# Normalising the two heads of a biased attention row on GpSimd and ScalarE at once, in a newly found order of steps

## The chip, the core and the metric

The kernel runs on one core of a Trainium2 chip. A core has TensorE (PE in the profile), VectorE (DVE), ScalarE (ACT), GpSimd (POOL) and SyncE (SP), which here only issues DMAs. The engines run side by side; each takes its own instructions strictly in the order in which they were written, and semaphores hold them back where one needs another's result. The metric is the device time of one launch in microseconds (us). Before the change it is 2065.31 us, the median of 3 runs (2063.07 to 2065.85).

## The reference

Four layers are applied to 8 items of 512 tokens by 256 features, in float32, each to the layer-normalised input and added to it: a causal attention with rotary embedding (16 heads of 16), a gated layer, a biased attention, and the gated layer again.

```python
x = L0_attn_a_x
x = x + _L0_attn_a_ref(_layernorm(x, axis=-1), ...)   # layer 0, causal
x = x + _L0_ffn_ref(_layernorm(x, axis=-1), ...)      # layer 1, gated
x = x + _L0_attn_b_ref(_layernorm(x, axis=-1), ...)   # layer 2, biased
x = x + _L0_ffn_ref(_layernorm(x, axis=-1), ...)      # layer 3, gated
```

The gated layer takes the half of the tokens with the highest gate value, runs an attention over them alone, and writes gate times result back to their places. The change is in the biased attention, 16 heads of 64:

```python
scores = jnp.einsum('bhid,bhjd->bhij', q, k) * scale
rel = jnp.arange(t)[None, :] - jnp.arange(t)[:, None] + (t - 1)
bias = rel_bias[rel]
scores = scores + bias.transpose(2, 0, 1)[None]
attn = jax.nn.softmax(scores, axis=-1)
out = jnp.einsum('bhij,bhjd->bhid', attn, v)
```

## The kernel before

The work is cut into steps, named by kind, item s, layer l and two numbers n and q. Kinds that begin with c_ belong to the causal layer, f_ to the two gated ones, b_ to the biased one. Items overlap: while the biased layer of item s runs, the last gated layer of item s-1 and the causal and first gated layer of item s+1 run between its steps. Only the first two items' first layers and the last item's last layer have little or nothing beside them.

In the biased layer n is one of 8 pairs of heads (128 features). b_q, b_k and b_v project the pair. A row is one of the four tiles of 128 queries (q) against all 512 keys, for both heads of the pair, so there are 4 x 8 x 8 = 256 rows. For each row:

- b_row: PE makes the scores of the two heads (L1669, two matmuls, recorded as four), DVE adds the band of biases and takes the maximum (L1394), negates it (L1399), and ACT takes the exponential in place and its sum (L1203), the two heads one after the other;
- b_nrm: DVE takes the reciprocal of the two sums (L1403); POOL multiplies the row of each head by it, in place, the first head and then the second (L1114), and raises norm_done after the second;
- b_tr: PE waits for norm_done, transposes the row (L1677, four transposes for each head, into two PSUM banks), and ACT copies each bank to PT (L1212).

After four rows b_val multiplies by the values (L1687) and b_y projects the output (L1448). Six rows are held in SBUF in probs; their exponentials, their normalised values and what PE transposes are all the same memory.

In the other layers, DVE takes maxima from PSUM (L1303 causal, L1377 gated), ACT takes exponentials from PSUM (L1176 into PTc, L1183 into PTf), PE makes scores from tiles of 32 rows (L1507, L1531, L1602, L1624), and L955 is a helper that records the matmuls of many steps.

Which step comes next is decided once, when the program is built, by a planner (in_order, L578). WORK gives for each kind of step what it costs on which engine; PLACE gives each step a due time, with a row of numbers for each kind in each stage of the run ("first", "cycle", "last" and so on); of the steps whose inputs are done, the one with the lowest due time is next. All engines, and SP's queue of loads for band and wb, follow this one list, each leaving out the steps in which it has no part. The planner also assigns the 8 PSUM banks, which PE takes back when ACT or DVE has read them. Where it reckons that PE will stand idle for long, the kernel writes filler transposes of an identity (L1464 to L1468); there are 636 of them.

PE works with tiles of several shapes: b_row uses two tiles of 64 rows, b_val two of 64 columns, the causal and gated attention steps tiles of 32, the rest the full array. TILES tells the planner which. Its order of before has 1760 steps with work on PE, in which the shape changes 737 times from one step to the next.

Of the kernel before, what the change touches and what calls it, by code (L numbers as in the profile page):

```python
# [9 lines left out]
ALU = mybir.AluOpType  # L10
# [11 lines left out]
PAIRS = H // 2  # L22
# [68 lines left out]
    "norm": {"b_nrm": 1},  # L91
}


def raised(sem, step):
# [42 lines left out]
    "b_nrm": [("dve", 0.065), ("pool", 0.667), ("pool", 0.667)],  # L138
# [46 lines left out]
def wait_for(x, y):  # L185
# [5 lines left out]
    if x.kind == "f_spread" and y.kind == "f_rank":  # L191
# [7 lines left out]
    ("cycle", "b_k"): [3550, -20290, 1306, 4062, 4436, 4140, 4696, 5305],  # L199
    ("cycle", "b_ln"): [1262],  # L200
    ("cycle", "b_nrm"): [2638, 3695, 3640, 3225, -20356, 4054, 2981, 2909, 4109, 4148, 4021, 2935, 4375, 3948, -23318,
        -23114, 4742, 3629, 5013, -4314, -23816, -10443, -23404, 5301, -23338, 5234, 5291, 5573, 4071, -23111, 5627,
        5525],
    ("cycle", "b_q"): [3196, -17363, 2209, 4150, -23317, -23105, -23313, 3727],
    ("cycle", "b_row"): [3568, 2483, 3386, 3576, -17334, 3747, 2880, 3676, 3538, 4356, 3997, 3970, 4036, -22757, 3966,
        -23319, 4525, 3836, -25665, -22838, -23399, 5250, -23127, -23029, 4951, 3629, 4299, 5506, 5521, -4078, 5564,
        5149],
    ("cycle", "b_tr"): [3737, 3899, 1936, 4069, 3053, 4259, 4296, 4109, 3959, -22860, 4110, -22481, -22974, 3923, 4021,
        4492, 5069, 5153, -22477, -21082, -22759, 5270, -6484, 5410, -4078, 5475, 5685, 5028, -18270, 5713, 5715,
        5508],  # L210
    ("cycle", "b_v"): [2826, 3562, 4101, 4300, -23336, 4743, -22759, 3751],
    ("cycle", "b_val"): [4383, 3998, -25042, 4071, 4069, 4022, 3918, 3906, 4617, 4618, -23312, -22775, 3980, 4682,
        -22433, 3910, 5411, -465, -18750, 1128, 5520, -15222, 2450, 5594, 5767, -18026, 5803, 5964, 6117, -23816, 6150,
        4297],
    ("cycle", "b_xt"): [3453],
    ("cycle", "b_y"): [6185, 6257, 5046, 6298],
    ("cycle", "c_dk"): [751, 1735],
    ("cycle", "c_dq"): [-9876, 1178],
    ("cycle", "c_hk"): [-25692, -26122],
    ("cycle", "c_hm"): [1900, 2381],  # L220
    ("cycle", "c_k"): [-25283, 1133],
    ("cycle", "c_ln"): [1596],
    ("cycle", "c_m"): [1231, 2224],
    ("cycle", "c_p1"): [1685, 1880, 825, 1812, 1814, 1835, -26435, 1988, 2283, -25667, 2225, 2342],
    ("cycle", "c_p2"): [-25857, -26620, 2189, -25905, 824, 2403, -31973, -25731, -31999, -31998, 824, -21029],
    ("cycle", "c_q"): [-25895, -1117],
    ("cycle", "c_rq"): [-25876, -25667],
    ("cycle", "c_v"): [1822, 1723],
    ("cycle", "c_va"): [2315, -21553, -26065, -25931, -26140, 2122],
    ("cycle", "c_vb"): [2425, 2341, -21554, 2451, 1708, -27849],  # L230
    ("cycle", "c_xq"): [1304, 1931],
    ("cycle", "c_xt"): [-26366],
    ("cycle", "c_y"): [2558, -27782],
    ("cycle", "f_gate"): [-4118],
    ("cycle", "f_gather"): [2758],
    ("cycle", "f_hk"): [-32246],
    ("cycle", "f_hm"): [-26272, 1112],
    ("cycle", "f_k"): [2803],
    ("cycle", "f_ln"): [-26583],
    ("cycle", "f_m"): [2974, 3174],  # L240
    ("cycle", "f_o"): [3364],
    ("cycle", "f_p1"): [2909, 2146, 2968, 2936],
    ("cycle", "f_p2"): [3157, 3207, 2714, 2145],
    ("cycle", "f_part"): [2341],
    ("cycle", "f_q"): [2876],
    ("cycle", "f_rank"): [2715],
    ("cycle", "f_row"): [2637],
    ("cycle", "f_rq"): [2714],
    ("cycle", "f_spread"): [3210],
    ("cycle", "f_v"): [2878],  # L250
    ("cycle", "f_va"): [3304, 3314],
    ("cycle", "f_vb"): [2818, 1878],
    ("cycle", "f_xq"): [2888],
    ("cycle", "f_y"): [3420, -26301],
    ("cycle3", "f_gate"): [6360],
    ("cycle3", "f_gather"): [6449],
    ("cycle3", "f_hk"): [5867],
    ("cycle3", "f_hm"): [6300, 6916],
    ("cycle3", "f_k"): [6624],
    ("cycle3", "f_ln"): [5519],  # L260
    ("cycle3", "f_m"): [6911, 6955],
    ("cycle3", "f_o"): [7115],
    ("cycle3", "f_p1"): [6841, 6842, 6893, 6912],
    ("cycle3", "f_p2"): [6915, 7004, 6752, 6788],
    ("cycle3", "f_part"): [3988],
    ("cycle3", "f_q"): [6615],
    ("cycle3", "f_rank"): [6377],
    ("cycle3", "f_row"): [5019],
    ("cycle3", "f_rq"): [5082],
    ("cycle3", "f_spread"): [6920],  # L270
    ("cycle3", "f_v"): [6818],
    ("cycle3", "f_va"): [7050, 7068],
    ("cycle3", "f_vb"): [6789, 6751],
    ("cycle3", "f_xq"): [6691],
    ("cycle3", "f_y"): [7172, 6817],
    ("first", "b_k"): [-3531, -5724, -3283, 2755, 15934, 11053, 13316, 7847],
    ("first", "b_ln"): [19106],
    ("first", "b_nrm"): [4611, 2091, 1400, 2970, 3511, 5654, 3829, 1690, 13396, 12728, 14614, 13159, 13289, 2911,
        13060, 13182, 10760, 8545, 8998, 14183, 19693, 11177, 12395, 10720, 3549, 18717, 9584, 18285, 13795, 15430,
        1912, -2429],  # L280
    ("first", "b_q"): [-3868, 2912, 9237, 10023, 11107, 15038, 11335, 16171],
    ("first", "b_row"): [2066, -8171, -4615, -4092, 4637, 2120, 11108, -3532, 2394, 11989, 452, 14111, -11398, 2393,
        8880, 2483, 22791, 8981, 8681, 17105, 3780, 2091, 18708, 6192, 7207, 14652, 6343, 20826, -20208, 4895, 2428,
        526],
    ("first", "b_tr"): [9594, 8800, 4897, 6030, 11633, 4802, 11088, 8568, 13585, 11130, 17050, 10988, 11759, 12828,
        2458, 4136, 14548, 8343, 15354, 19160, 9814, 5419, 9782, 13226, -11880, -1040, -13485, 1333, 4379, 2513, 500,
        5883],
    ("first", "b_v"): [1892, 1604, 11176, 13174, 11234, 11205, 9730, -2031],
    ("first", "b_val"): [10070, 10259, 1988, -7921, 12048, 3827, 4102, 10300, 23781, 5884, 9581, 13207, 10682, 9717,
        8728, 8281, 20971, 11416, 19627, 1555, -20843, 3036, 5244, 3443, -2922, 5941, 5044, 3662, 3462, -9064, 1504,  # L290
        2778],
    ("first", "b_xt"): [22969],
    ("first", "b_y"): [6325, -11860, 5440, 710],
    ("first0", "c_dk"): [282, 2428],
    ("first0", "c_dq"): [-456, -545],
    ("first0", "c_hk"): [-25531, 3679],
    ("first0", "c_hm"): [4148, 2481],
    ("first0", "c_k"): [-7624, -69],
    ("first0", "c_ln"): [-171702],
    ("first0", "c_m"): [4163, 5008],  # L300
    ("first0", "c_p1"): [3589, 3764, 3598, 3598, 3583, 3597, 4158, 4157, -161523, 4003, 4374, 4002],
    ("first0", "c_p2"): [3779, 3930, 1994, 4059, 3953, 3597, 3925, 5275, 4394, 2837, 5214, 3732],
    ("first0", "c_q"): [-8701, -161419],
    ("first0", "c_rq"): [-13080, -11293],
    ("first0", "c_v"): [1491, 3301],
    ("first0", "c_va"): [4609, 3463, 4766, 6280, 3950, 5711],
    ("first0", "c_vb"): [5046, 3489, 2415, 6523, 2581, 4747],
    ("first0", "c_xq"): [1538, 3952],
    ("first0", "c_xt"): [3964],
    ("first0", "c_y"): [6944, 3550],  # L310
    ("first0", "f_gate"): [3590],
    ("first0", "f_gather"): [5264],
    ("first0", "f_hk"): [1650],
    ("first0", "f_hm"): [3715, 6506],
    ("first0", "f_k"): [3478],
    ("first0", "f_ln"): [7065],
    ("first0", "f_m"): [6900, 10182],
    ("first0", "f_o"): [13088],
    ("first0", "f_p1"): [4295, 3631, 7445, 4795],
    ("first0", "f_p2"): [1941, 9074, 10136, 9959],  # L320
    ("first0", "f_part"): [8357],
    ("first0", "f_q"): [5263],
    ("first0", "f_rank"): [7410],
# [12 lines left out]
    ("first1", "c_k"): [3874, 2319],
    ("first1", "c_ln"): [-161544],
# [389 lines left out]
def hybrid_kernel(nc, x_in, wqk_a, wv_a, wo_a, w_b, wo_b, band_in, wg_f, wq_f, wk_f, wv_f, wo_f,  # L727
                  cos_in, sin_in, sides_in, out):
    with ExitStack() as ctx:
# [14 lines left out]
        def sem(name):  # L744
            return ctx.enter_context(nc.semaphore(name))
# [1012 lines left out]
```

## Time and profile before

| | |
|---|---|
| median of 3 runs | 2065.31 us (2063.07 to 2065.85) |
| the profiled execution | 2064.3 us, of which 2062.3 us are the span of the profile |
| PE, weight loads of PE | 1996.6 us (97%), 1282.7 us (62%) |
| DVE, ACT, POOL | 1514.8 us (73%), 1155.7 us (56%), 693.0 us (34%) |
| TensorE clock granted | 0.997 of full speed |

Busy times are shares of the span. PE counts as busy while a matmul is under way by the profile's model of its end, and PEld, the loading of the next weights, overlaps it. The engines' shares don't add up to one another, since they run at the same time.

### The profile page before, as it was taken

What the parts mean: (1) busy time and instruction counts of PE and PEld (TensorE: products, weight loads), DVE (VectorE), ACT (ScalarE), POOL (GpSimd) and SP (SyncE); (2) the same over time, 40 slices, a digit from 0 to 9 for tenths busy, and PEclk for the clock granted to TensorE, in tenths of its full rate; (3) what the DMA queues carried; (4) which work ended last, traced back from release to release, by engine and by line L of the source; (5) the groups of instructions that cost most, each with busy time, mean ns of one, the idle gap of its engine ahead of it and who ended that gap; (6) DMA issues with size and microseconds to landing.
All of it is one profiled execution on the core that took longest, in us unless ns stands there. A gap on an engine that the chain in (4) does not pass through costs nothing.

```text
span 2062.3 us, 42104 instructions
## 1 busy us (share of the span) xinstructions
PE 1996.6 (97%) x16080; PEld 1282.7 (62%) x16080; DVE 1514.8 (73%) x4803; ACT 1155.7 (56%) x2578; POOL 693.0 (34%) x879
## 2 busy tenths in 40 slices
PE   8999999999999999999999999999999999999998
PEld 6676666655666555765566555765566655675567
DVE  8977654877868877778778697686876877857446
ACT  2545763766637475474745657465663766627742
POOL 6323242253313342233523333234341243414220
PEclk9999999999999999999999999999999999999999
DMA  3001211120111111121011211012110120102200
GB/s 146 2 1 35 70 60 59 45 90 19 60 31 63 57 35 44 35 84 43 31 37 52 72 42 45 19 60 72 34 62 10 52 90 17 62 16 70 69 1 21
DMA packets 29062, 98.77 MB, mean 48 GB/s; under 512 B 2880, under 2 KB 11200, under 8 KB 28736
## 3 DMA queue, kind: packets, MB, share of 16 engines
q1 hardware_dynamic: 28864, 96.09, 14.0%
q8 instruction: 129, 2.11, 0.4%
q14 instruction: 69, 0.57, 0.1%
HBM read 91.89 MB, written 4.19 MB: 47 GB/s over the span
## 4 chain that ended last, share of the span: by engine, by line
PE 73%; DVE 17%; ACT 6%; issue 2%; POOL 1%; DVEq 0%
PE ps L955 21%; PE ps L1687 10%; PE ps L1448 10%; PE ps L1677 9%; PE ps L1669 8%; DVE ps L1303 5%; DVE probs L1394 5%; PE ps L1531 3%; ACT PTc L1176 3%; PE ps L1636 2%; DVE peaks L1377 2%; PE ps L1624 2%; PE ps L1545 2%; PE ps L1602 2%; PE ps L1507 2%
## 5 line engine op out<-in xcount | busy, mean ns | idle before, releaser
L1114 POOL TENSOR_SCALAR probs<-probs,rtotal 128x512 f32<-128x512 f32 x512 | 345.5, 695 | 556.5 <-DVE rtotal L1403 555.9
L1203 ACT ACTIVATE probs<-probs,peak 128x512 f32<-128x512 f32 x512 | 365.0, 714 | 156.3 <-DVE peak L1399 155.6
L1394 DVE CUSTOM_DVE_ANT_0 probs<-ps,band 128x512 f32<-128x512 f32 x512 | 332.5, 687 | 61.1 <-PE ps L1669 61.1
L1212 ACT ACTIVATE PT<-ps 128x512 f32<-128x512 f32 x512 | 262.4, 618 | 45.7 <-PE ps L1677 45.7
L1677 PE MATMUL ps<-ident,probs 128*128 128x128 f32 x2048 | 249.5, 275 | 1.6 <-POOL probs L1114 1.2
L1677 PEld LDWEIGHTS ps<-ident,probs 128*128 128x128 f32 x2048 | 225.2, 141 | 39.3 <-issue 28.3
L1303 DVE CUSTOM_DVE_ANT_0 ps<-ps,later 128x512 f32<-128x512 f32 (+3 forms) x512 | 232.7, 526 | 16.5 <-PE ps L1507 16.3
L1669 PE MATMUL ps<-KT,QT 64*128 64x512 f32 x1024 | 242.9, 606 | 0.0
L1687 PE MATMUL ps<-PT,Vb 128*64 128x512 f32 x1024 | 239.6, 601 | 0.0
L955 PE MATMUL ps<-xnT,wb 128*128 128x512 f32 x512 | 233.5, 598 | 0.6 <-ACT xnT L1139 0.6
L1176 ACT ACTIVATE PTc<-ps 128x384 f32<-128x384 f32 (+1 forms) x384 | 167.7, 550 | 40.6 <-PE ps L1531 39.8
L1377 DVE TENSOR_REDUCE peaks<-ps 128x2 f32<-128x512 f32 x256 | 156.7, 681 | 21.2 <-PE ps L1602 21.2
L955 PEld LDWEIGHTS ps<-xnT,wb 128*128 128x128 f32 x512 | 93.1, 190 | 108.5 <-issue 100.7
L1106 POOL TENSOR_SCALAR_AFFINE_SELECT PTc<-PTc 128x512 f32<-128x512 f32 x128 | 81.4, 648 | 234.0 <-ACT PTc L1176 233.7
L1669 PEld LDWEIGHTS ps<-KT,QT 64*128 64x128 f32 x1024 | 94.1, 186 | 92.1 <-issue 72.0
L1077 POOL TENSOR_TENSOR rstd<-veps,pow_half 128x2 f32<-128x2 f32 x64 | 46.8, 734 | 308.8 <-DVE veps L1234 308.7
L1183 ACT ACTIVATE PTf<-ps 128x512 f32<-128x512 f32 x256 | 130.4, 616 | 29.4 <-PE ps L1624 28.8
L1687 PEld LDWEIGHTS ps<-PT,Vb 128*64 128x64 f32 x1024 | 65.5, 136 | 126.8 <-issue 113.3
L955 PEld LDWEIGHTS ps<-wb,xnT 128*128 128x128 f32 x1024 | 121.3, 192 | 16.6 <-issue 12.7
L955 PE MATMUL ps<-wb,xnT 128*128 128x128 f32 x1024 | 126.2, 277 | 0.0
L1448 PE MATMUL ps<-wob,OTb 128*128 128x256 f32 x512 | 113.7, 379 | 0.0
L1448 PEld LDWEIGHTS ps<-wob,OTb 128*128 128x128 f32 x512 | 96.4, 190 | 12.6
(156 smaller groups left out, 3348.9 us busy)
## 6 DMA issues: line engine op xcount, KB each, us to landing
band<-in_band SPq DMA_DIRECT2D x64, 896.0 KB, 4.5
wb<-in_w_b SPq DMA_DIRECT2D x64, 384.0 KB, 3.1
x<-in_x SPq DMA_DIRECT2D x16, 256.0 KB, 3.0
out<-x SPq DMA_DIRECT2D x16, 256.0 KB, 2.2
wob<-in_wo_b SPq DMA_DIRECT2D x1, 1024.0 KB, 8.5
wqk<-in_wqk_a SPq DMA_DIRECT2D x1, 512.0 KB, 5.7
cos_t<-in_cos SPq DMA_DIRECT2D x1, 256.0 KB, 5.2
sin_t<-in_sin SPq DMA_DIRECT2D x1, 256.0 KB, 6.1
```

Of the source, the lines that this page charges most:

```text
L955: last = nc.tensor.matmul(o, w, r, start=(i == 0), stop=(i == len(pairs) - 1))
L1114: last = g.tensor_scalar(unit, unit, rtotal[:, r % 8, e:e + 1], 1.0, ALU.mult, ALU.mult)
L1176: a.activation(pt_c(m, q)[:, h], bank(now, name)[:, 0:w], ACT.Exp, scale=float(DH) ** -0.5).then_inc(act_read, 1)
L1203: last = a.activation(unit, unit, ACT.Exp, bias=peak[:, r % 8, e:e + 1], accum_out=total[:, r % 8, e:e + 1])
L1212: a.activation(PT[:, k % 2, e, :, tile_of(q)], bank(now, name).rearrange("p (k n) -> p k n", k=NT), ACT.Copy).then_inc(act_read, 1)
L1303: last = v.tensor_tensor_reduce(out=scores, in0=scores, in1=later[:, NT * P - w:NT * P], scale=1.0, scalar=-3e38, op0=ALU.add, op1=ALU.max ...
L1377: v.tensor_reduce(places[:, h:h + 1].rearrange("p h t -> p (h t)"), bank(now, name).rearrange("p (t n) -> p t n", t=NS), AXIS.X, ALU.max). ...
L1394: v.tensor_tensor_reduce(out=probs[:, r % ROWS_HELD, e, :], in0=bank(now, name), in1=band[:, k % 2, e, lo:lo + T], scale=1.0, scalar=-3e38 ...
L1448: last = te.matmul(o[:, j * D:(j + 1) * D], w, r, start=(k == 0 and j == 0), stop=(k == count - 1 and j == 1))
L1669: full(te.matmul(bank(now, name), QT2[half(e), k % 2, tile_of(q)], KT2[half(e), k % 2, :], start=True, stop=True), now, name)
L1677: last = te.transpose(bank(now, name)[:, tile_of(t)], probs[:, r % ROWS_HELD, e, tile_of(t)], ident[:])
L1687: last = te.matmul(o[half(e), :], Vb[:, k % 3, q, half(e)], PT[:, k % 2, e, q, :], start=(q == 0), stop=(q == NT - 1))
```

## The change

Three things are changed. In b_nrm POOL multiplies the first head alone and raises norm_done after it. ACT multiplies the second head, with an activation of the kind Copy and the reciprocal as its scale, and raises the new semaphore norm_second_done. In b_tr PE waits for norm_done ahead of the first head's transposes, and for norm_second_done ahead of the second head's. The planner's cost of b_nrm follows: 0.667 on POOL and 0.53 on ACT, both from the end of DVE's reciprocal. And all of PLACE is replaced, so that every engine's order is another. No other line changes; the sizes, buffers and DMAs are the same.

```diff
@@ RAISES
     "norm": {"b_nrm": 1},
+    "norm_second": {"b_nrm": 1},
@@ WORK
-    "b_nrm": [("dve", 0.065), ("pool", 0.667), ("pool", 0.667)],
+    "b_nrm": [("dve", 0.065), ("pool", 0.667), ("act", 0.53, 0)],
@@ PLACE (207 rows of numbers, nearly every number replaced; one of them)
-    ("cycle", "b_k"): [3550, -20290, 1306, 4062, 4436, 4140, 4696, 5305],
+    ("cycle", "b_k"): [3435, -7470, -1963, 4088, 4623, -12784, 5024, 5326],
@@ gpsimd
                         if kind == "b_nrm":
                             r = (PAIRS * s + n) * NT + q
                             pool.wait_ge(rtotal_done, plan.after("rtotal", now, now))
-                            for e in range(2):
-                                unit = probs[:, r % ROWS_HELD, e, :]
-                                last = g.tensor_scalar(unit, unit, rtotal[:, r % 8, e:e + 1], 1.0, ALU.mult, ALU.mult)
-                            last.then_inc(norm_done, 1)
+                            unit = probs[:, r % ROWS_HELD, 0, :]
+                            g.tensor_scalar(unit, unit, rtotal[:, r % 8, 0:1], 1.0, ALU.mult, ALU.mult).then_inc(norm_done, 1)
@@ scalar
+                        if kind == "b_nrm":
+                            r = (PAIRS * s + n) * NT + q
+                            act.wait_ge(rtotal_done, plan.after("rtotal", now, now))
+                            unit = probs[:, r % ROWS_HELD, 1, :]
+                            a.activation(unit, unit, ACT.Copy, scale=rtotal[:, r % 8, 1:2]).then_inc(norm_second_done, 1)
@@ tensor
                         if kind == "b_tr":
                             pe.wait_ge(norm_done, plan.after("norm", Step("b_nrm", s, l, n, q), now))
                             for e, name in enumerate(names(now)):
+                                if e == 1:
+                                    pe.wait_ge(norm_second_done, plan.after("norm_second", Step("b_nrm", s, l, n, q), now))
                                 room(now, name)
```

## Rows read from the trace of the kernel before

**Rows 1.** the page: span, busy time and share of each engine, then the chain that ended last.

```profile
span 2062.3 us, 42104 instructions
...
PE 1996.6 (97%) x16080; PEld 1282.7 (62%) x16080; DVE 1514.8 (73%) x4803; ACT 1155.7 (56%) x2578; POOL 693.0 (34%) x879
...
PE 73%; DVE 17%; ACT 6%; issue 2%; POOL 1%; DVEq 0%
```

**Rows 2.** stretches: us, busy (count) of PE PEld DVE ACT POOL, clock, DMA share, GB/s.

```profile
180.00:1989.00 1809.00, 1763.41 (x13737) 1106.24 (x13737) 1324.55 (x4202) 1068.85 (x2401) 619.38 (x789) 1.00 0.15 50
0.00:180.00 180.00, 166.91 (x1740) 119.47 (x1741) 150.57 (x504) 72.72 (x150) 67.08 (x84) 0.99 0.12 43
1989.00:2062.30 73.30, 66.24 (x605) 56.97 (x605) 39.64 (x100) 14.15 (x27) 6.53 (x6) 0.98 0.05 15
```

**Rows 3.** the same stretches, the filler transposes of L1468 alone.

```profile
180.00:1989.00 1809.00, 10.32 (x72) 7.97 (x72) 1.00 0.15 50
0.00:180.00 180.00, 50.61 (x367) 41.96 (x367) 0.99 0.12 43
1989.00:2062.30 73.30, 24.44 (x197) 21.67 (x197) 0.98 0.05 15
```

**Rows 4.** waits of PE in the middle: total us, times, longest.

```profile
PE ps L1602 <- DVE Vx L1370: 7.6, 6, 1.3
PE ps L1531 <- ACT PTc L1176: 6.9, 18, 0.6
...
PE ps L1507 <- ACT PTc L1176: 5.5, 12, 0.7
...
PE ps L1677 <- POOL probs L1114: 1.2, 1, 1.2
...
PE ps L955 <- ACT xnT L1139: 0.6, 2, 0.3
```

**Rows 5.** waits of PE's weight loader for POOL's rows, whole span.

```profile
PEld ps L1677 <- POOL probs L1114: 5.5, 15, 1.4
```

**Rows 6.** groups by line: busy us, mean ns of one, idle time before, its releaser.

```profile
L1114 POOL TENSOR_SCALAR probs<-probs,rtotal 128x512 f32<-128x512 f32 x512 | 345.5, 695 | 556.5 <-DVE rtotal L1403 555.9
...
L1288 DVE SCALAR_TENSOR_TENSOR X<-Dq,sides,X 128x1024 fp32r<-128x1024 f32 x16 | 26.2, 1638 | 0.0
...
L1139 ACT ACT_TABLE_LOAD x1 | 1.3, 1283 | 0.8 <-PEq L1751 0.8
```

**Rows 7.** ACT's copies from SBUF: a pair, then ns min/median/max of all.

```profile
460.87 1.14 ACT L1162 ACTIVATE HI<-LOf 128x512 fp32r<-128x512 f32 x2
...
L1162 ACT ACTIVATE HI<-LOf x32: 612/617/757, 25.1 to 1700.3; 128x512 fp32r<-128x512 f32 x32
```

**Rows 8.** DVE's X by line: ns min/median/max.

```profile
L1288 DVE SCALAR_TENSOR_TENSOR X<-Dq,sides,X x16: 1274/1278/2249, 24.9 to 1713.1; 128x1024 fp32r<-128x1024 f32 x16
```

**Rows 9.** the chain that ended last: start us, us, what (records).

```profile
1956.66 5.35 PE ps L1669 x24
...
1972.79 1.92 PE ps L1669 x8
```

**Rows 10.** timelines of DVE, ACT and POOL near 880 us.

```profile
878.45 4.86 DVE L1377 TENSOR_REDUCE peaks<-ps 128x2 f32<-128x512 f32 x8
...
883.72 0.28 DVE L1403 RECIPROCAL rtotal<-total 128x2 f32<-128x2 f32 x3
...
879.31 0.18 ACT L1203 ACTIVATION_READ_ACCUMULATOR probs<-probs,peak 128x1 f32 x1
881.37 0.60 ACT L1191 ACTIVATE KT<-ps 128x512 f32<-128x512 f32 x1 [1.87 <-PE ps L955]
...
883.98 4.02 POOL L1114 TENSOR_SCALAR probs<-probs,rtotal 128x512 f32<-128x512 f32 x6 [7.47 <-DVE rtotal L1403]
```

**Rows 11.** the chain in the tail: one of its smallest pieces.

```profile
2011.14 0.02 issue
```

**Rows 12.** the page's DMA issues: times, KB each, us to landing.

```profile
band<-in_band SPq DMA_DIRECT2D x64, 896.0 KB, 4.5
```

More of the change, by code:

```diff
@@ L215 @@
[L215 to L225, printed above, removed]
@@ L266 @@
[L266 to L280, printed above, removed]
@@ L281 @@
[L281 to L287, printed above, removed]
@@ new lines @@
+    ("cycle", "c_hm"): [2225, 2330],
+    ("cycle", "c_k"): [-12486, 1499],
+    ("cycle", "c_ln"): [1606],
+    ("cycle", "c_m"): [-2585, -14270],
+    ("cycle", "c_p1"): [2025, 2188, -15529, 1858, 1934, 2040, -9868, 1333, 2296, -2899, 1475, 2329],
+    ("cycle", "c_p2"): [-4243, 1061, 2249, -12846, -6788, 2334, -15367, -13218, -12847, -8145, -13216, -7286],
+    ("cycle", "c_q"): [-16052, -312],
+    ("cycle", "c_rq"): [-15002, 2035],
+    ("cycle", "c_v"): [2038, 1825],
+    ("cycle", "c_va"): [2308, -8145, -13003, -6858, -4262, -4243],
@@ new lines @@
+    ("cycle", "c_vb"): [2346, -2556, 2328, 2443, -15368, -15649],
+    ("cycle", "c_xq"): [1187, 2241],
+    ("cycle", "c_xt"): [-15814],
+    ("cycle", "c_y"): [2526, -15569],
+    ("cycle", "f_gate"): [2743],
+    ("cycle", "f_gather"): [2860],
+    ("cycle", "f_hk"): [-4243],
+    ("cycle", "f_hm"): [-1457, -4072],
+    ("cycle", "f_k"): [2902],
+    ("cycle", "f_ln"): [2669],
+    ("cycle", "f_m"): [3049, 3145],
+    ("cycle", "f_o"): [3356],
+    ("cycle", "f_p1"): [970, -4071, 2996, 2990],
@@ new lines @@
+    ("cycle", "f_p2"): [3074, 3146, -2282, -9563],
+    ("cycle", "f_part"): [-6176],
+    ("cycle", "f_q"): [2914],
+    ("cycle", "f_rank"): [2765],
+    ("cycle", "f_row"): [-6455],
+    ("cycle", "f_rq"): [-4070],
+    ("cycle", "f_spread"): [2844],
+    ("cycle", "f_v"): [2949],
+    ("cycle", "f_va"): [3155, 3206],
+    ("cycle", "f_vb"): [-1296, -1427],
+    ("cycle", "f_xq"): [2981],
+    ("cycle", "f_y"): [3374, -1280],
+    ("cycle3", "f_gate"): [1352],
+    ("cycle3", "f_gather"): [6589],
@@ new lines @@
+    ("cycle3", "f_hk"): [3577],
+    ("cycle3", "f_hm"): [6822, 6847],
+    ("cycle3", "f_k"): [6780],
+    ("cycle3", "f_ln"): [-12714],
+    ("cycle3", "f_m"): [6949, 7057],
+    ("cycle3", "f_o"): [7109],
+    ("cycle3", "f_p1"): [6850, 6885, 6965, 7025],
+    ("cycle3", "f_p2"): [7024, 7025, 6669, 6834],
+    ("cycle3", "f_part"): [-4482],
+    ("cycle3", "f_q"): [6768],
+    ("cycle3", "f_rank"): [6549],
+    ("cycle3", "f_row"): [6377],
+    ("cycle3", "f_rq"): [-5416],
+    ("cycle3", "f_spread"): [7056],
@@ new lines @@
+    ("cycle3", "f_v"): [6847],
+    ("cycle3", "f_va"): [7067, 7094],
+    ("cycle3", "f_vb"): [7049, -17709],
+    ("cycle3", "f_xq"): [6787],
+    ("cycle3", "f_y"): [7147, 7188],
+    ("first", "b_k"): [-1065, -1065, 2493, 8512, 8530, 13415, 10676, 13406],
+    ("first", "b_ln"): [14272],
+    ("first", "b_nrm"): [4333, -5684, 5453, 3282, 8373, 9636, 7705, 10030, 10313, 7438, 18458, 17358, 14356, 6849,
+        14169, 13676, 22252, 16372, 6647, 13294, 10007, 11510, 3078, 17094, 13247, 9705, 14329, 16050, 7259, 11662,
+        1844, 1162],
@@ new lines @@
+    ("first", "b_q"): [-817, 1227, 6086, 12164, 13405, 6025, 15843, 8843],
+    ("first", "b_row"): [1826, -3269, 4650, 850, 6488, -1607, 7508, 3584, 13072, 243, 9610, -533, 5959, 19029, 6446,
+        13022, 22195, 21714, 16822, 1917, 10496, -3392, 14758, 939, 15612, 6215, -2422, 1205, 12000, -10774, 2675,
+        596],
+    ("first", "b_tr"): [6706, 3843, 8583, -838, 2261, 11725, 12691, -1531, 14828, 18226, 19625, 6364, 13281, 16505,
+        14075, -676, 6365, 7034, 18829, 6705, 10214, -4311, 9872, 9371, 1409, -10064, -1433, 1952, 3293, -1304, -1319,
+        -4355],
@@ new lines @@
+    ("first0", "f_p2"): [8354, 3583, 3062, 7043],
+    ("first0", "f_part"): [8666],
+    ("first0", "f_q"): [3605],
+    ("first0", "f_rank"): [8169],
+    ("first0", "f_row"): [7776],
+    ("first0", "f_rq"): [6184],
+    ("first0", "f_spread"): [9113],
+    ("first0", "f_v"): [7825],
+    ("first0", "f_va"): [10501, 13518],
+    ("first0", "f_vb"): [1045, 12664],
+    ("first0", "f_xq"): [8958],
+    ("first0", "f_y"): [14355, 16943],
+    ("first1", "c_dk"): [4497, 6105],
+    ("first1", "c_dq"): [4655, 5442],
@@ new lines @@
+    ("first1", "c_hk"): [4358, 7117],
+    ("first1", "c_hm"): [7206, 8204],
+    ("first1", "c_k"): [500, 3726],
+    ("first1", "c_ln"): [-159660],
+    ("first1", "c_m"): [8915, 6585],
+    ("first1", "c_p1"): [5447, 7965, 8487, 5834, 6321, 3390, 4168, 7748, 8552, 7207, 8852, 5673],
+    ("first1", "c_p2"): [-2824, 5142, 3629, 4466, 7556, 6124, 4096, 8536, 13871, 4849, 7251, 8352],
+    ("first1", "c_q"): [-3337, 3323],
+    ("first1", "c_rq"): [5027, 5702],
+    ("first1", "c_v"): [1250, 3327],
@@ new lines @@
+    ("first1", "f_p1"): [10063, -2356, 12178, 13145],
+    ("first1", "f_p2"): [12989, 14484, 11183, -178990],
+    ("first1", "f_part"): [-1166],
+    ("first1", "f_q"): [7825],
+    ("first1", "f_rank"): [4065],
+    ("first1", "f_row"): [-1028],
+    ("first1", "f_rq"): [4404],
+    ("first1", "f_spread"): [13399],
+    ("first1", "f_v"): [7320],
+    ("first1", "f_va"): [18293, 19046],
+    ("first1", "f_vb"): [11999, 19190],
+    ("first1", "f_xq"): [9655],
+    ("first1", "f_y"): [22463, 19520],
@@ new lines @@
+    ("last", "b_k"): [9465, 12699, 8665, 15467, 19714, 9212, 14108, 11677],
+    ("last", "b_ln"): [10139],
+    ("last", "b_nrm"): [14576, 8068, 6457, 2280, 23009, 7605, 12456, 20576, 16753, 9940, 9464, 8394, 8146, 9099, 12273,
+        32984, 12025, 1191, 9888, 15379, 16752, 763, 3677, 16548, 19509, 489, 527, 7011, 20869, 853, 4146, 697],
+    ("last", "b_q"): [6025, 5794, 6139, 1353, 23004, 3193, 13984, 20515],
+    ("last", "b_row"): [15632, -2324, 8952, 1192, 3601, -5620, 19445, 2472, 1046, 3678, 31998, 2880, 6974, 7677, 4782,
+        10938, 15602, -3235, 6289, 11646, -36, 18315, 11427, 20704, 36073, 446, 1208, 1350, 2486, 2325, 19200, 2484],
@@ new lines @@
+    ("last", "b_xt"): [23619],
+    ("last", "b_y"): [18206, 434, 434, 4842],
+    ("last1", "f_gate"): [2330],
+    ("last1", "f_gather"): [1878],
+    ("last1", "f_hk"): [2082],
+    ("last1", "f_hm"): [487, 1823],
+    ("last1", "f_k"): [434],
+    ("last1", "f_ln"): [1828],
+    ("last1", "f_m"): [2220, 18177],
+    ("last1", "f_o"): [2063],
+    ("last1", "f_p1"): [556, 476, 2323, 1824],
+    ("last1", "f_p2"): [678, 3067, 2498, -422],
+    ("last1", "f_part"): [42336],
+    ("last1", "f_q"): [3058],
@@ new lines @@
+    ("last1", "f_rank"): [18160],
+    ("last1", "f_row"): [434],
+    ("last1", "f_rq"): [18205],
+    ("last1", "f_spread"): [654],
+    ("last1", "f_v"): [18324],
+    ("last1", "f_va"): [18166, 485],
+    ("last1", "f_vb"): [20724, 1376],
+    ("last1", "f_xq"): [20580],
+    ("last1", "f_y"): [2219, 17392],
+    ("last2", "f_gate"): [11761],
+    ("last2", "f_gather"): [1775],
+    ("last2", "f_hk"): [2668],
+    ("last2", "f_hm"): [21820, 34587],
+    ("last2", "f_k"): [16364],
+    ("last2", "f_ln"): [1067],
@@ new lines @@
+    ("last2", "f_m"): [26744, 9673],
+    ("last2", "f_o"): [38638],
+    ("last2", "f_p1"): [25703, 23008, 30463, 33533],
+    ("last2", "f_p2"): [32514, 31950, 7208, 17221],
+    ("last2", "f_part"): [5717],
+    ("last2", "f_q"): [21323],
+    ("last2", "f_rank"): [13293],
+    ("last2", "f_row"): [8977],
+    ("last2", "f_rq"): [6968],
+    ("last2", "f_spread"): [1134],
+    ("last2", "f_v"): [21867],
+    ("last2", "f_va"): [36026, 36110],
+    ("last2", "f_vb"): [19081, -993],
+    ("last2", "f_xq"): [7136],
@@ L429 @@
+    ("last2", "f_y"): [40788, 434],
 }
```

266 lines of the change are left out of this document (70 added, 196 removed).

## Prediction

> **What bounds the kernel now.** I read the page's busy shares first: TensorE (PE) is busy 97% of the span, VectorE (DVE) 73%, ScalarE (ACT) 56%, GpSimd (POOL) 34%; the chain that ended last is 73% PE [rows 1]. The change speeds up something on the engine with the most room. So the question is not how long a normalisation takes, but how much of PE's time hangs on it.
>
> Next I cut the span where the biased layer begins and ends, by the windows view [rows 2], and asked the same windows for the filler transposes of L1468 alone [rows 3]. Slack of PE is idle time plus filler:
> - head, 0 to 180 us, before the first biased row: 180.0 - 166.9 = 13.1 idle, 50.6 filler, 63.7 in all;
> - middle, 180 to 1989 us, where all 256 rows are: 1809.0 - 1763.4 = 45.6 idle, 10.3 filler, 55.9 in all;
> - tail, 1989 to 2062.3: 73.3 - 66.2 = 7.1 idle, 24.4 filler, 31.5 in all.
>
> The step b_nrm is in the middle alone. Head and tail can move only because the order is another.
>
> Third, the waits of PE in the middle [rows 4]: the seven ACT rows, from PTc at L1531 (6.9) down to xnT (0.6), add to 18 us, eight DVE rows, from Vx at L1370 (7.6) down, to 18 too, and POOL's normalised rows cost PE one wait of 1.2 us. The weight loader waits for POOL's rows 15 times, 5.5 us in all [rows 5]; such a wait shows on PE only where no matmul runs beside it. That is all that a faster normalisation could take away directly.
>
> **The change part by part.** (a) *POOL loses 256 of its 512 multiplications.* One takes 695 ns [rows 6] and six in a row take 4.02 us, 0.67 each [rows 10]. POOL's busy time falls by 256 x 0.67 = 172 us, and the second head of a row is no longer 0.67 us behind the first. What PE gains is between 1.2 us (its own wait) and 1.2 + 5.5 = 6.7 us (all of the loader's too). I take 3: most loader waits run beside a matmul.
>
> (b) *ACT gains 256 copies with a scale, SBUF to SBUF.* The nearest rows are its 128x512 copies from SBUF at L1162: 617 ns for one in the middle of 32, 1.14 us for two, so each further one costs 0.53 us [rows 7]. 256 x 0.53 = 136 us, and ACT goes from 1155.7 to some 1292 us, 63% of the span. No new table load comes with it: one load stands in the whole trace, though Exp and Copy alternate all along [rows 6]. In the middle ACT is busy 1068.9 of 1809 us, 59%; with 136 more it is 67%, below DVE's 73% (1324.6). So no engine replaces PE as the bound of the middle. But the ACT waits of PE are 18 us, and work in front of PTc and PTf in ACT's queue makes them longer. In proportion to busy time (+13%) that is 2.3 us; if every wait of PE on ACT grew by half, 9. I take 3.
>
> (c) *ACT gains a wait.* Before its copy it waits for the reciprocal of L1403, and its queue is in order: behind it stand exponentials of PTc and PTf, copies of transposed banks, K and V, whose banks PE wants back. How late can the reciprocal be? In the stretch around 880 us ACT has finished the last exponentials at 879.5; DVE is in eight reductions of L1377 until 883.3 and finishes the reciprocals at 884.0, so POOL waited 7.47 us [rows 10]. ACT's next copies, KT and PT, started at 881.37. With b_nrm ahead of them they would start at 884.0 + 3 x 0.53 = 885.6, 4.2 us late. That is the old place of the step. Laid side by side along the planner's order of before, the traced times of ACT and DVE show 164 of 256 rows whose reciprocal is there when ACT would reach the copy; in 92 ACT would wait, mostly under 1 us, at most 4.7. A new order can put the step later. Price: from 0, if it always does, to the slower rival below; I take it as 0 in the sum, because ACT idles 41% of the middle.
>
> (d) *PE gains a wait between the two heads of a transposed row.* It follows four transposes. Where ACT keeps up, the semaphore is up already. The nearest rows are the waits that b_row takes between its own two matmuls, and there a row costs 0.86 us with no gap [rows 9]. Bounds 0 and, if each showed as the smallest "issue" piece of the chain does, 256 x 0.02 = 5 us [rows 11]; I take 0.
>
> (e) *Less contention between POOL and DVE.* The rows show some: X at L1288 takes 1274 ns at best, 1278 in the middle and 2249 at worst, 16 times, with a sum of 26.2 us, so 26.2 - 16 x 1.274 = 5.8 us were lost [rows 6, 8]. But that is rare, and some of it is met by POOL operations that stay. Bounds 0 and 5.8 us; I take 1. The Trainium skill, page "SBUF — State Buffer", section "Who interferes with whom", says that GpSimd and a DVE instruction in a 2-port mode or with two SBUF inputs exclude each other for a whole instruction, while ACT waits for nobody. By X's maximum the trace agrees, by its median such meetings are few, and by the rule at its fullest the sum would gain the 5.8 instead of the 1.
>
> (f) *The order of steps.* All 207 lists of due times are replaced, nearly every number in them, so each engine's queue is another one. SP's queue moves along: its 64 loads of band land 4.5 us after issue [rows 12], and no engine waits for band in the waits of before; two pairs lie between issue and use, so I cost them at nothing, and at up to 4.5 us each where that cover fails. What can an order be worth on PE? The chain near the end shows it [rows 9]: b_row steps (four records each) in a run of two take 1.92 us and in a run of six 5.35, which is (5.35 - 1.92) / 4 = 0.86 us for a row plus 0.20 for each visit to that tile shape. In the planner's order of before, the 1760 steps of PE change tile shape 737 times: about 737 x 0.20 = 147 us, more than all idle time. So the order has 147 us of changes, 55.9 of slack in the middle and 95.2 of slack at the ends to play with. Rows that are ready 0.67 us earlier can be transposed in longer runs. If runs grow by 5%, 37 visits go: 7.4 us. An order that happened to be 5% worse loses as much. I take a gain of 7, the term with the least behind it: it rests on the shorter chain and the emptier POOL giving the order more freedom than ACT's load takes.
>
> **Sum.** -3 (a) +3 (b) +0 (c) +0 (d) -1 (e) -7 (f) = -8 us. The profiled execution took 2064.3 us (2062.3 span), 1.0 below the median of 2065.31 of the runs shown. 2064.3 - 8 = 2056.3; moved to the median, 2057.
>
> **The rivals.** *The changes cancel.* POOL costs PE 1.2 us directly, and a row is ready only when the later of two engines is done; ACT's in-order queue may hand over the second head no sooner than POOL did, so the change doesn't do what it says. What is left is an order of equal quality: 2065, or 2061 to 2069. For it speaks that POOL is among the smallest entries of PE's waits [rows 4]; against it, that no two orders share their visits and gaps. The Trainium skill, page "Perfetto Trace Analysis", section "Identifying Performance Opportunities", says that improving a kernel generally means improving its most-contended engine; by that rule moving POOL's work gives nothing but what the order brings. The trace agrees as far as the 1.2 us go.
>
> *ACT blocks behind DVE: slower.* Place: b_nrm on ACT in the six biased layers, of items 1 to 6, that share PE with a causal and two gated layers. In each round of before there would be the delay of 4.2 us worked out in (c) and, by the same reading, one of 2.1: 6.3 us, in six rounds 38 us of late ACT work. If a third of it reaches PE (an assumption: PE is full there, but has other steps at hand), it is +13 us, with the rest of the sum at 0: 2078. It decides once ACT is more than about 1.3 us late (PE's largest wait in these rows, that for Vx, is 1.3), because the four banks of an f_p2 or c_p2 step are then missed one after another. For it: ACT already makes PE wait for 18 us. Against it: 41% idle time on ACT and 164 of 256 rows without a wait.
>
> *The order brings much more.* Visits fall by 10% (15 us), and the ends lose a tenth of their 95 us: 2064.3 - 25 + 1 = 2040. For it: the ends hold more slack than the middle. Against it: their chains run through single steps of one item (PE, then DVE, then PE), which no order shortens.
>
> **Chances.** Forecast, 2045 to 2061: 0.40. Much more, around 2040: 0.10. Cancel, 2061 to 2069: 0.20. ACT blocks, around 2078: 0.30. About 0.2% (4 us) is what a measurement of this kernel can tell from no change. So faster 0.50, same 0.20, slower 0.30. The forecast's own range is 2045 to 2061. Eight in ten reaches to 2040 less the few microseconds of (e) and down-turned (b), 2038, and on the other side past the slower rival by (d)'s bound of 5 us, rounded down, 2082.
>
> **What the profile after would show.** (a) POOL near 520 us busy with 256 multiplications; no PE wait on POOL's rows in the middle. (b) ACT near 1290 us, a copy at about 0.62 us; PE's waits on PTc and PTf between 18 and 27 us. (c) A new row "ACT probs <- DVE rtotal": below 60 us in total the slower rival is dead, above 150 it is likely. (e) X's mean falls towards 1.28 us. (f) The middle's length against 1809 us, the head's against 180, the tail's against 73.3, the filler count against 636, and the loader's "issue" waits, which fall with the number of shape changes. The forecast is wrong if the middle does not shrink while ends stay; if all of the gain is in head or tail, (f) was right by luck and its reason wrong.

## The result, and the profile after

The changed kernel takes 2077.62 us (median of 4 runs, 2076.10 to 2079.41) against 2064.19 (median of 4, 2062.61 to 2065.85) for the kernel before: 1.0066 times as long, 95% interval 1.0054 to 1.0078. It is slower by 13.4 us, where 2057 was forecast. The time is close to the 2078 of the slower rival; whether the reason is too is what the experiments had to show.

The page of the kernel after, its span, busy times and the chain that ended last; the rows of before are [rows 1]:

```profile
span 2074.3 us, 42374 instructions
...
PE 1999.5 (96%) x16111; PEld 1285.2 (62%) x16111; DVE 1505.6 (73%) x4803; ACT 1299.4 (63%) x2834; POOL 523.8 (25%) x623
...
PE 57%; DVE 24%; ACT 12%; issue 2%; POOL 2%; DVEq 0%
```

ACT rose by 143.7 us and POOL fell by 169.2, as the change says. PE is hardly busier (2.9 us), so of the 12.0 us of span 9.1 are idle time of PE. The chain runs through PE for 57% of the span, no longer for 73%: it steps over to DVE and ACT more often.

Where in time did they come? Every item's first reciprocal marks a place that both traces have. Timelines of DVE, the marks of items 2 and 3, first the kernel before, then after:

```profile
611.14 0.17 DVE L1403 RECIPROCAL rtotal<-total 128x2 f32<-128x2 f32 x1
...
858.93 0.17 DVE L1403 RECIPROCAL rtotal<-total 128x2 f32<-128x2 f32 x1
```

```profile
613.77 0.17 DVE L1404 RECIPROCAL rtotal<-total 128x2 f32<-128x2 f32 x1
...
864.13 0.17 DVE L1404 RECIPROCAL rtotal<-total 128x2 f32<-128x2 f32 x1
```

A round lasts 250.4 us in place of 247.8. Read so for all items:

| stretch (between first reciprocals) | before, us | after, us | difference |
|---|---|---|---|
| start to item 1 | 363.4 | 363.4 | 0.0 |
| five rounds, items 1 to 5 | 5 x 247.8 | 5 x 250.4 | +13.0 |
| item 6's round | 259.7 | 261.8 | +2.1 |
| item 7 and the tail | 200.4 | 197.2 | -3.2 |

Before item 1 nothing is lost, at the end something is won, and all of the loss sits in the rounds, 2.6 us in each of five and 2.1 in that of item 6. One such round by the windows view, then the filler transposes in it alone (columns as in [rows 2] and, for the fillers, PE and its loader). First before, then after:

```profile
611.10:858.90 247.80, 240.69 (x1941) 151.26 (x1939) 189.29 (x600) 144.45 (x324) 86.37 (x108) 1.00 0.15 48
...
611.10:858.90 247.80, 1.58 (x11) 1.22 (x11) 1.00 0.15 48
```

```profile
613.80:864.10 250.30, 241.97 (x1951) 152.89 (x1949) 187.66 (x600) 162.17 (x355) 65.25 (x76) 1.00 0.14 47
...
613.80:864.10 250.30, 3.11 (x21) 2.27 (x21) 1.00 0.14 47
```

PE is idle 8.3 us of the round in place of 7.1, and spends 1.5 us more on fillers, which the kernel writes where its planner reckons a wait of over 1 us. So about half of the loss is waiting that the planner of the new order saw coming, and the other half idle time beside it. The waits of PE in the kernel after (total us, times, longest) over the whole span; [rows 4] has those of the middle before:

```profile
PE ps L1612 <- DVE peaks_r L1317: 6.0, 12, 0.6
PE ps L1532 <- ACT PTc L1172: 5.1, 20, 0.3
PE ps L953 <- ACT xnTc L1135: 5.0, 6, 0.8
PE ps L1559 <- DVE gate L1343: 4.9, 7, 0.7
PE ps L1508 <- DVE peaks L1304: 4.5, 14, 0.5
PE ps L1670 <- DVE QT L1384: 4.4, 6, 0.7
```

The waits on PTc, of which I had been afraid, are shorter than before (over the whole span 5.1 and 4.2 us, in place of 7.4 and 5.8); those on Vx and on POOL's rows are gone. In their place stand waits that hardly existed, mostly on DVE: peaks_r, the gate, QT. None has to do with a normalised row. From 180 to 1989 us the waits of PE on DVE add up to 27.6 us in place of 17.9, those on ACT to 19.8 in place of 18.2. ACT does wait for the reciprocal (waits of ACT, after):

```profile
ACT probs L1178 <- DVE rtotal L1404: 52.0, 23, 4.7
```

### The profile page after: what moved, and what is told of

Same layout as the page of the kernel before. It is cut to its first block, busy times and chain, and to the rows that moved or that the text cites. A ratio compares the mean times of both kernels' runs of the same rounds, so it can differ in the third digit from the quotient of the medians.

```text
span 2074.3 us, 42374 instructions
## 1 busy us (share of the span) xinstructions
PE 1999.5 (96%) x16111; PEld 1285.2 (62%) x16111; DVE 1505.6 (73%) x4803; ACT 1299.4 (63%) x2834; POOL 523.8 (25%) x623
## 4 chain that ended last, share of the span: by engine, by line
PE 57%; DVE 24%; ACT 12%; issue 2%; POOL 2%; DVEq 0%
PE ps L953 14%; PE ps L1449 9%; PE ps L1670 7%; PE ps L1690 7%; PE ps L1680 6%; DVE ps L1304 5%; DVE probs L1395 5%; DVE peaks L1378 4%; ACT probs L1204 3%; PE ps L1532 3%; ACT PTf L1184 3%; PE ps L1546 2%; ACT PTc L1172 2%; PE ps L1637 2%; ACT PT L1213 2%
## 5 line engine op out<-in xcount | busy, mean ns | idle before, releaser
L1111 POOL TENSOR_SCALAR probs<-probs,rtotal 128x512 f32<-128x512 f32 x256 | 180.6, 721 | 658.4 <-DVE rtotal L1404 658.4
L1178 ACT ACTIVATE probs<-probs,rtotal 128x512 f32<-128x512 f32 x256 | 168.8, 723 | 52.0 <-DVE rtotal L1404 52.0
```

## The experiments

Two theories stood at the start. O: the newly found order alone costs the time, the split in it is harmless. A: ACT's queue, standing behind DVE's reciprocal and longer by the copies, costs it. The first two runs cross the two parts of the change; all times are medians, all ratios are to the kernel before on the same chip.

**The split alone, in the old order.** The kernel before, its WORK and PLACE untouched, with the split in the instructions:

```diff
 pool, b_nrm:   -for e in range(2): ... last.then_inc(norm_done, 1)
                +first head alone, .then_inc(norm_done, 1)
 act, b_nrm:    +act.wait_ge(rtotal_done, plan.after("rtotal", now, now))
                +a.activation(unit, unit, ACT.Copy, scale=rtotal[:, r % 8, 1:2]).then_inc(norm_second_done, 1)
 pe, b_tr:      +if e == 1: pe.wait_ge(norm_second_done, ...)
```

> The order of steps, the banks and the fillers of before, and only the split: ACT multiplies the second head at the place of b_nrm in its queue, PE waits for both. Theory A (ACT's queue stands behind DVE's reciprocal): slower than before by 13 us at least, and than the changed kernel too, since this order was made with b_nrm costing ACT nothing: 2080 to 2110 us, with a row 'ACT probs <- DVE rtotal' above 100 us in all. Theory O (the newly found order alone is to blame, the split is harmless): 2060 to 2066 us.

Measured: 2148.59 us, 1.0407 (1.0392 to 1.0423), 84 us slower than before. So the split is not harmless: in the order that stood, it costs six times what the whole change costs, and more than theory A allowed. ACT's wait for the reciprocal, which A wanted above 100 us, is 55.2. PE's three largest waits in this run:

```profile
PE ps L1607 <- ACT PT L1217: 18.9, 8, 4.0
PE ps L1536 <- ACT Vb L1201: 12.7, 6, 2.1
PE ps L1607 <- DVE gX L1293: 9.4, 6, 1.6
```

**The new order alone, both heads on POOL.** The kernel after with the five edits of the instructions taken back, WORK and PLACE untouched.

> The order, banks and fillers of the changed kernel, and both heads on POOL again. Theory O: the loss stays, 2076 us or more, and a little more still since the order was made for rows that are ready 0.67 us sooner: up to 2090. Theory A: ACT is freed of 144 us and of its wait for the reciprocal, so most of the 13 us come back: 2062 to 2070 us.

Measured: 2076.16 us, 1.0055 (1.0040 to 1.0070). The loss stays. Its rounds take 250.1 us, those of the kernel after 250.4. The new waits of PE are there without the split, so they came with the order:

```profile
PE ps L1607 <- DVE peaks_r L1312: 7.0, 12, 0.7
...
PE ps L1554 <- DVE gate L1338: 5.0, 7, 0.7
...
PE ps L1665 <- DVE QT L1379: 4.4, 6, 0.7
```

Crossed:

| | both heads on POOL | second head on ACT |
|---|---|---|
| order of before | 2064 | 2149 |
| new order | 2076 | 2078 |

Within the new order the split is worth nothing that can be told (1.5 us slower, less than the intervals). The 12 us are the order's, taken with the PSUM banks and the fillers that the planner derives from it. But that order is not a mistake beside the change: it is what keeps the split from costing 84.

**The copy without its scale, in the changed kernel.** The second head is not normalised here.

```diff
-a.activation(unit, unit, ACT.Copy, scale=rtotal[:, r % 8, 1:2]).then_inc(norm_second_done, 1)
+a.activation(unit, unit, ACT.Copy).then_inc(norm_second_done, 1)
```

> The changed kernel, but ACT's copy has no scale: the second head of each row is not normalised. It waits and writes as before. Measures what the pointer to the reciprocal costs: mean of one should fall from 723 to about 617 ns, three in a row from 1.95 to about 1.7 us. Were the mis-sized copy the cause, 256 x 0.1 = 26 us less on ACT bring 3 to 10 us back (2068 to 2074). Theory O: 1 us or less.

Measured: 2074.80 us, 1.0048 (1.0031 to 1.0065): 2.8 us of the 13 come back at the medians, though the two intervals overlap. ACT's timeline, three copies in a row, first in the kernel after, then here:

```profile
525.25 1.95 ACT L1178 ACTIVATE probs<-probs,rtotal 128x512 f32<-128x512 f32 x3
```

```profile
403.75 1.72 ACT L1178 ACTIVATE probs<-probs 128x512 f32<-128x512 f32 x3
```

A copy that takes its scale from a column costs (1.95 - 0.71) / 2 = 0.62 us, one without (1.72 - 0.61) / 2 = 0.55 (0.71 and 0.61 are single ones). The difference of some 0.07 to 0.1 us is real, for 256 of them 18 to 26 us of ACT's time (its busy time fell by 23.2 us), and it is worth little.

**No wait for the reciprocal, in the changed kernel.** The second head is not normalised here either.

```diff
-act.wait_ge(rtotal_done, plan.after("rtotal", now, now))
+act.wait_ge(exp_done, plan.after("exp", Step("b_row", s, l, n, q), now))
-a.activation(unit, unit, ACT.Copy, scale=rtotal[:, r % 8, 1:2]).then_inc(norm_second_done, 1)
+a.activation(unit, unit, ACT.Copy, scale=sides[:, 0:1]).then_inc(norm_second_done, 1)
```

> The changed kernel, but ACT's copy scales by a constant column and waits for its own exponential in place of DVE's reciprocal: the second head is not normalised. Takes away the stop of ACT's queue behind DVE (52 us in 23 waits in the changed kernel) and leaves the copy's time. Theory A: 5 to 13 us come back (2064 to 2072). Theory O: 2074 to 2078.

Measured: 2077.33 us, 1.0061 (1.0046 to 1.0076). The 52.0 us of waiting are gone from ACT, and no time came back: the rounds still take 250.4 us. In the new order A is out. ACT waits there where nobody needs it.

**The fillers of the middle taken out, after and before.** The condition that writes them now asks for the stages of head and tail:

```diff
-if kind != "c_xt" and wait > (0.4 if ends else 1):
+if kind != "c_xt" and ends and wait > 0.4:
```

> The changed kernel without the filler transposes of the middle (stages cycle, cycle3, first, last; those of head and tail stay). The changed kernel has 21 of them a round, before has 11, and PE's busy time of a round is 1.3 us longer, 10 x 0.137 us. If fillers stand in PE's way: 6 rounds x up to 2.9 us, 5 to 17 us come back (2060 to 2072). If they only fill waits: 2076 to 2079, same round of 250.4 us.

> The kernel before without the filler transposes of the middle, the counterpart. If fillers stand in PE's way: 3 to 9 us faster than before. If they only fill waits: within 2 us of 2064.

Measured: the kernel after without them 2088.43 us, 1.0123 (1.0108 to 1.0138); the kernel before 2069.20, 1.0023 (1.0013 to 1.0033). Both got slower, by about 11 and 5 us, where I had asked only whether they get faster. The fillers fill waits, and do one thing more. The cores view, mean granted clock, of the kernel after without them:

```profile
core 0: 2088.8 us, clock 0.988
```

With them it is 0.999; in the kernel before it is 0.994 without and 0.997 with them. So the extra fillers are a sign of the new order's waits and not their cause, and the waits are dearer without them.

**What the split costs in the old order: wait or copy?** Twice the 84 us case, once without the wait (the edit of the run without it, above), once with the wait and a copy of 16 of the 512 columns. The second head is not normalised in the first, and only in 16 columns in the second.

```diff
-unit = probs[:, r % ROWS_HELD, 1, :]
+unit = probs[:, r % ROWS_HELD, 1, 0:16]
```

> The split in the old order (2148.6 us), but ACT's copy waits for its own exponential in place of DVE's reciprocal and scales by a constant column: the second head is not normalised. If the 84 us come from ACT standing behind DVE, most go: 2070 to 2090. If they come from the 0.63 us of each copy in a place of the queue where PE waits for a bank: 2125 to 2150.

> The split in the old order, with the wait for the reciprocal, but ACT's copy takes 16 of the 512 columns (the rest of the second head is not normalised), about 0.2 us in place of 0.63. If the wait is what costs: 2120 to 2150. If the copy's time is: 256 x 0.4 = 100 us less on ACT, and 2070 to 2100.

Measured: without the wait 2102.14 us, 1.0188 (1.0173 to 1.0203); with the short copy 2094.92, 1.0153 (1.0136 to 1.0170). Each alone costs 38 and 31 us, both together 84. The first result lies between my two alternatives, the second within the range for the copy's time. Neither wait nor copy makes up the cost by itself, and the short copy is not free: one takes 293 ns, and ACT is 46 us busier than in the kernel before. That the sum is more than its parts because the delays add up on ACT before they reach PE is argued, not shown. Part of it goes with the clock: the mean granted clock is 0.987 with both, 0.994 without the wait and 0.993 with the short copy, against 0.997 before.

**The split for 18 rows.** Only the rows of [rows 10], three in each of the six rounds, in the otherwise unchanged kernel before.

```diff
+SPLIT = {("cycle", 5), ("cycle", 6), ("cycle", 7)}
 pool, b_nrm:   +for e in range(1 if on_act(now) else 2):
 act, b_nrm:    +if kind == "b_nrm" and on_act(now):
 pe, b_tr:      +if e == 1 and on_act(now):
```

> The kernel before in every respect but 18 of the 256 rows: rows 1 to 3 of the second pair (n=1) in the six rounds, the burst near 880 us, where the reciprocals come 4.5 us after ACT's last exponential. Only there ACT multiplies the second head. By the reading of the trace of before ACT's next copy is 4.2 us late in each round, and PE is reached because the banks of the transposed rows come late: between 6 x 2 = 12 and 6 x 4.2 = 25 us, so 2076 to 2089. If ACT's delay is absorbed by PE's other steps: 2064, within 2 us.

Measured: 2101.60 us, 1.0177 (1.0160 to 1.0194). 18 copies cost 37.8 us, 6.3 in each round, more than my upper bound of 4.2. The timeline of ACT in the second of these rounds:

```profile
638.33 0.19 ACT L1220 ACTIVATION_READ_ACCUMULATOR probs<-probs,peak 128x1 f32 x1
642.93 1.95 ACT L1194 ACTIVATE probs<-probs,rtotal 128x512 f32<-128x512 f32 x3 [4.41 <-DVE rtotal L1420]
644.78 0.57 ACT L1208 ACTIVATE KT<-ps 128x512 f32<-128x512 f32 x1
645.26 2.04 ACT L1229 ACTIVATE PT<-ps 128x512 f32<-128x512 f32 x4
```

The timeline of PE beside it:

```profile
640.19 1.91 PE L1696 MATMUL ps<-ident,probs 128*128 128x128 f32 x16
646.09 0.59 PE L1619 MATMUL ps<-gLO,gX 32*128 32x256 f32 x4 [3.99 <-ACT PT L1229]
```

ACT is done at 638.5, stands 4.41 us for DVE, makes three copies, and only then copies KT and PT; PE, whose next step needs the bank that PT empties, stands for 3.99 us. That is the 4.2 of the prediction. The other 2.3 show in the windows view of the same stretch, two microseconds to a row, with the granted clock as the third number from the end:

```profile
642.00:644.00 2.00, 0.10 (x1) 0.00 (x0) 0.88 (x6) 1.07 (x2) 1.01 (x2) 1.00 0.00 0
644.00:646.00 2.00, 0.00 (x0) 0.00 (x0) 0.00 (x0) 2.00 (x5) 1.02 (x2) 0.79 0.00 0
646.00:648.00 2.00, 1.91 (x19) 1.72 (x20) 0.68 (x2) 1.30 (x3) 0.00 (x0) 0.50 0.00 0
648.00:650.00 2.00, 2.00 (x12) 2.00 (x11) 1.80 (x4) 0.00 (x0) 0.00 (x0) 0.50 0.04 8
650.00:652.00 2.00, 2.00 (x19) 1.67 (x22) 0.00 (x0) 0.87 (x2) 0.00 (x0) 0.50 0.00 0
652.00:654.00 2.00, 1.92 (x41) 1.54 (x38) 1.58 (x3) 0.88 (x2) 0.00 (x0) 1.00 0.60 197
```

While PE stood, the clock granted to it went from 2.4 to 1.2 GHz (1.00 to 0.50), and stayed there for some 6 us after it had work again; at half speed that is up to 3 us of work not done. The stop comes in all six rounds, 3.99 to 4.02 us long, but the half clock isn't the same in each. The ten microseconds after the stop in the first and the second round:

```profile
392.50:402.50 10.00, 9.77 (x112) 7.46 (x114) 7.15 (x14) 4.61 (x10) 1.36 (x2) 0.83 0.14 41
646.00:656.00 10.00, 9.74 (x83) 7.53 (x84) 6.00 (x12) 4.24 (x9) 0.93 (x2) 0.70 0.13 41
```

In the first, third and fifth round a mean of 0.83 means 3.4 us at half clock, in the others it is 5 to 6 us (0.69 to 0.74). The first and the fifth round are longer than before by 5.8 and 5.6 us, the second and the fourth by 6.7 and 6.5. (The third, 6.8, loses clock a second time, at 1000 us; the sixth, 5.7, is held against a round of before that lost some too.) So a stop of 4.0 us cost 5.6 to 6.8, and 6.3 on average.

**The split for 125 rows where ACT has time.** The same kernel with another set: 14 of the 32 rows of each round, 23 of item 0, 18 of item 7.

```diff
-SPLIT = {("cycle", 5), ("cycle", 6), ("cycle", 7)}
+SPLIT = {("cycle", 0), ("cycle", 9), ("cycle", 10), ..., ("last", 29)}   # 55 places, 125 rows
```

> The kernel before, but ACT multiplies the second head in 125 other rows (14 of the 32 of each round, 23 of item 0, 18 of item 7), those in whose places the planner's reckoning of the old order sees ACT idle long enough. ACT gains 125 x 0.62 = 78 us, POOL loses 84. If what counts is whether the copy stands in front of work that PE waits for, and not ACT's load: within 3 us of before (2061 to 2067). If ACT's load counts: a share of the 84 us that the whole split cost in this order, near half, 2090 to 2106.

Measured: 2064.71 us, 1.0007 (0.9997 to 1.0016). 125 copies on ACT cost nothing that can be told from no change (a round takes 248.1 us, 0.3 more), 18 others cost 38 us. It is the place in the queue that counts: ACT waits for the reciprocal 1.7 us in all here, and 26.5 us in the run with 18 rows. It gains nothing either, though POOL lost 81.5 us.

**The copy later in ACT's queue, old order.** A step of its own, b_cpy, for the copy; it stands 1 to 24 steps behind b_nrm.

```diff
 RAISES: +"norm_second": {"b_cpy": 1},
 WORK:   -"b_nrm": [("dve", 0.065), ("pool", 0.667), ("pool", 0.667)],
         +"b_nrm": [("dve", 0.065), ("pool", 0.667)],
         +"b_cpy": [("act", 0.63)],
 act:   +if kind == "b_cpy":     # placed by LATER[stage, row] steps behind b_nrm of the old order
```

> The split for all 256 rows in the old order, with ACT's copy as a step of its own, put later in ACT's queue than b_nrm where that delays nothing (places searched for each of the 32 rows of a round, of item 0 and of item 7; all other steps in the order of before). If the 84 us came from the copies' places alone: 2064 to 2072. If the old order has no room on ACT for 159 us more, wherever they stand: 2080 to 2095.

Measured: 2079.87 us, 1.0071 (1.0056 to 1.0086). 68 of the 84 us are gone; ACT's wait for the reciprocal falls to 0.4 us. All other steps stand in the old order, but the copies are not the only difference: the planner reckoned with their cost here, so it dealt out the PSUM banks anew and wrote 700 fillers in place of 636. How much of the 68 us is owed to that is not shown. 16 us remain, so in the places that I tried the old order hasn't room for all 256 copies; other places were not run. By this way the split costs about what it costs by the new order.

**Split and new order at the ends alone.** The due times of after and the split for items 0 and 7, the due times of before and POOL for the six rounds between.

```diff
+SPLIT = ("first", "last")
 PLACE: rows "cycle" and "cycle3" as before; "first", "first0", "first1", "last", "last1", "last2" as after
 WORK of b_nrm in the split stages: [("dve", 0.065), ("pool", 0.667), ("act", 0.63, 0)]
```

> The change in items 0 and 7 alone: the split and the new order (due times of the stages first, first0, first1, last, last1, last2) for 64 of the 256 rows, and for the six rounds between them the order of before with both heads on POOL. In the changed kernel item 0 ended where it did before, and the stretch after the last round was 3.2 us shorter, while the seven stretches between were 15.2 us longer. If the whole loss sits in the rounds: 2060 to 2065 us, and 1 to 3 us of gain at the end if that part is worth something by itself. If the loss came with the split wherever it stands: 64 / 256 of 13.4, 2067 or more.

Measured: 2066.47 us, 1.0007 (0.9998 to 1.0016). The rounds take 247.8 us again, and of the loss no more is left than 1.8 us against the kernel before on the same chip (2064.67), which the interval can't tell from nothing. The gain of the ends didn't last, though: the start to item 1 took 367.5 us here in place of 363.4, more than the shorter tail (198.7 in place of 200.4) gives back. No version that I ran beats the kernel before.

## Why the prediction was wrong

The sign is wrong, and the step that failed is (f). I gave the new order a gain of 7 us, reasoning that it has more freedom when rows are ready sooner; measured, the new order alone costs 12. The changes of tile shape did fall, from 737 to 717, but I priced each at 0.20 us, which should have given 4 us in all, some 0.5 in a round if they are spread evenly. PE's busy time of a round rose by 1.3 us where fillers explain 1.5; the 0.25 between them neither bears the price out nor refutes it, and it is small beside the 2.6 us lost. What rose was the waiting, planned and unplanned. The freedom went the other way: the order had to keep 256 more instructions on ACT out of PE's way. That this is why it is the poorer one is argued, not shown; shown is that it is poorer by 12 us with POOL and 13 with the split, and that the old one can't carry the split as it stands.

Part of this could have been worked out before any run, and the prediction leaves it out. The kernel's own planner adds up its costs without a chip. Worked out from the code of the two kernels, it reckons 2030.7 us for the kernel before and 2034.8 for the kernel after, with rounds of 245.0 and 246.0; 2094.6 for the old lists with the new cost of b_nrm, and 2041.0 for the new lists with the old cost. Against the kernel before that is +4, +64 and +10, where +13, +84 and +12 were measured: the sign is right each time. It doesn't see all of it, and the 6 us by which it prefers the new lists with the split to the same lists with POOL did not show (1.5 us the other way).

(a) was right in size and worthless in effect: POOL fell to 523.8 (forecast 520), PE's wait of 1.2 us on its rows is gone, and the loader's grew from 5.5 to 11.3 us. Of the 3 us taken, the runs show none: 125 rows without POOL's second multiplication changed nothing (though PE's one wait of 1.2 us was still there).

(b) was mis-sized by the row chosen. I took a copy without a scale column, 617 ns and 0.53 us; the trace of before also had one with a scale column, into X (1149 ns for 1024 columns), and exponentials from SBUF of 714 ns. Measured 723 ns and 0.62 us for each further one. ACT gained 143.7 us, for 136 forecast; PE's waits on PTc fell, and all its waits on ACT in the middle rose by 1.6 us where I took 3. As a share of the 13 us it is at most the 2.8 of the plain copy.

(c) is the step with the right mechanism in the wrong kernel. The 4.2 us read from three timelines are the 3.99 of the 18-row run, at the very place. I put a third of ACT's delay onto PE; in that place PE took nearly all of it, and about half as much again by the clock, which I had left out. In the changed kernel the mechanism costs nothing, as the run without the wait shows. So the slower rival's 2078 met the time by chance: its place and price are those of the old order, where it costs up to 84 us. Its threshold by which above 150 us of waiting for the reciprocal would confirm it and below 60 refute it was half right: 52.0 us and harmless in the new order, but 55.2 and ruinous in the old one. The sum of an engine's waits says nothing; who stands behind it does.

(d) was right at 0 in the new order, as the kernel with both heads on POOL and the kernel after differ by 1.5 us in all. (e) was right to be small: X's median stays at 1278 ns, and its worst case is 2289 in place of 2249.

"The changes cancel", with the split doing nothing for PE, is true of the split in the new order and of the 125 rows, and for its reason (PE's waits on POOL were the smallest entries) I should have given it more. It fails only in taking the order for neutral.

What stays open: where the planner's reckoning falls short (it sees 1.0 of the 2.6 us of a round, with its costs for the steps that wait on peaks_r, the gate and QT the same as before), and whether a longer search finds an order for the split as good as the old one is for POOL. Neither was tried on the chip.

## What to carry to other kernels

When PE is full and another engine's work is moved, ask of each moved instruction what is queued behind it and who waits for that; the total load of the engine, or the total of its waits, doesn't tell (18 copies cost 38 us, 125 others nothing that can be told). An order made by hand or by search belongs to the placement of work for which it was made: cross the two parts on the chip before either is credited or blamed. Where the order comes from a planner, ask it first what it reckons for each of the four. And expect little from a step for which PE hardly waits: it waited 1.2 us for POOL's rows, its loader 5.5, and taking half of POOL's work off 125 of them returned nothing.

## What the runs showed of the hardware

A stop of PE of 4 us among dense work halved the granted clock for 3.4 us after it in three of six rounds and for 5 to 6 in the others, and made the stop cost 5.6 to 6.8 us in place of 4. The 78 filler transposes of the middle are worth about 5 us in the kernel before (clock 0.997 with them, 0.994 without), and the 149 of the kernel after about 11 us (0.999 and 0.988), though they compute nothing. An ACT copy of 128x512 from SBUF to SBUF costs 0.07 to 0.1 us more with its scale in a column than without one.
